# First stage of an attention and FFN kernel: V weights loaded as float32 and cast by GpSimd, x four buffers deep, norms pipelined, second V group from tile 17

## The chip, the cores and the metric

One Trainium2 chip, all 8 cores. Two cores share one sequence of the batch of four: the even core of a pair runs one plan, the odd core another. The metric is device time in microseconds of the slowest core of an execution, and the median over several executions.

Engine names: PE is TensorE's matmuls, PEld its weight loads, DVE is VectorE, ACT is ScalarE, POOL is GpSimd, SP is SyncE, which here only starts DMAs.

## The reference

```python
def _L0_attn_ref(x, Wq, bq, Wk, bk, Wv, bv, Wo, bo):      # 16 heads of 128, causal
    q = jnp.einsum('btc,hcd->bhtd', x, Wq) + bq[None, :, None, :]
    k = ...; v = jnp.einsum('btc,hcd->bhtd', x, Wv) + bv[None, :, None, :]
    scores = jnp.einsum('bhtd,bhsd->bhts', q, k) * scale
    probs = jax.nn.softmax(scores + causal, axis=-1)
    y = jnp.einsum('bhts,bhsd->bhtd', probs, v)
    return y.transpose(0, 2, 1, 3).reshape(Bn, Tn, H * D) @ Wo + bo
...
x = x + _layernorm(_L0_attn_ref(_layernorm(x), Wq, bq, Wk, bk, Wv, bv, Wo, bo))
x = x + _layernorm(_L0_ffn_ref(_layernorm(x), weight, w_scale, bias))   # int8 weights, x quantized per token
```

x is 4 x 4096 x 2048 in float32. The change touches only the inner layernorm of x, its transposition and the product with Wv.

## The kernel before

Each core works on token tiles of 128 rows. The even core's plan holds 21 tiles (NK = 21) and computes the output of all of them; the odd core's plan holds 32 tiles (NK = 32) for keys and values and computes the output of 11. The slowest core is an even one.

**The first stage**, the one that the change touches, goes over the tiles t = 0, 1, 2, ... For each one:
- SP starts the load of 128 rows of x, float32, 1 MB, into one of three buffers `xin` (`load_x`);
- DVE takes the statistics (`x_stats`: four BATCH_NORM_STATS2 of 128x512, one BATCH_NORM_AGGREGATE into the only `mv`), then waits for ACT's square root in `c_sd`, then makes the reciprocal `c_rs` and the shift `c_nm`;
- ACT takes the square root (L909), normalizes the tile into `xln` (L914, 128x2048, bf16, two buffers) and, once PE has transposed it, copies two halves from PSUM into `xT` (L919);
- PE transposes the tile in 16 blocks (`transposes`, L694), one tile ahead of its products, and computes V for it (`v_job`, L708): 16 matmuls of 512 columns per group of four heads;
- DVE adds the bias and evicts it (`v_out`, L1065) and SP stores it to DRAM (`store_v`).

V has four groups of 512 columns. Groups 0 and 1 belong to the first stage: group 0 is computed for each tile as it comes, group 1 beside it from tile `V2_AT` on (10 here), and then for the tiles before `V2_AT`. After that come K and Q of head 0, V groups 2 and 3, and then the heads, one after another, and the FFN; in all of this PE works from `xT` and the later weights.

**Orders written out by hand.** Every engine has one list of instructions, so the place of a step in it decides what it waits behind. ACT's list for one tile is: square root of t, normalization of t, the two copies of t. DVE's is: `v_out(0, t)`, then the whole of `x_stats(t + 3)`. PE's is: transposes of t + 1, `v_job(0, t)`, and from `V2_AT` on `v_job(1, t)`. SP's is: `load_x(t + 4)`, `store_v(0, t)`. `ps` has two banks for V jobs, `xln` and the statistics behind `c_sd` one or two buffers.

**V weights.** They lie in DRAM as float32. GpSimd starts the DMAs of a group in four parts (`load_wv`, L585), each 1 MB in DRAM, which the DMA itself casts to bf16 on the way into `wv[0]` or `wv[1]`. Group 0's four are started when the first x tile has landed; group 1's four after normalizations 1, 3, 5 and 7; the weights of Q and K of head 0 (`load_wqk(0)`, L599 and L600, 2 MB in DRAM) right behind them.

Of the kernel before, what the change touches and what calls it, by code (L numbers as in the profile page):

```python
# [28 lines left out]
V2_AT = 10  # L29


class Plan:
# [177 lines left out]
    def frees(self, lo, hi):  # L210
# [29 lines left out]
        + ["x_in%d" % i for i in range(3)]  # L240
# [26 lines left out]
def build_nc():  # L267
# [26 lines left out]
    with contextlib.ExitStack() as top:  # L294
# [44 lines left out]
        xin = at("xin", [128, 3, C], F32, A + 32 * KB)  # L339
# [91 lines left out]
        def sync_program(sp, pl):  # L431
# [36 lines left out]
            def load_x(t):  # L468
                if t >= 3:
                    w.wait_ge("ln_a", t - 2)  # L470
                sp.dma_start(out=xin[:, t % 3, :], in_=x_seq[t * 128:(t + 1) * 128, :]
                             ).then_inc(S["x_in%d" % (t % 3)], 16)
# [18 lines left out]
            load_x(3)  # L491
            for t in range(NK):
                if t + 4 < NK:
                    load_x(t + 4)
# [84 lines left out]
        def gpsimd_program(g, pl):  # L579
# [103 lines left out]
        def tensor_program(pe, pl):  # L683
# [19 lines left out]
            def v_job(grp, t):  # L703
                b = open_job(pl.job_no[("v", grp, t)])
                w.wait_ge("tp_ev", 2 * t + 2)
                for kc in range(KC):
                    w.wait_ge("wv%d%d" % (grp % 2, kc // 4), 16 * (grp // 2 + 1))
# [194 lines left out]
        def scalar_program(a, pl):  # L902
            w = Seen(a, S)
            NK, NQ, NC, N = pl.NK, pl.NQ, pl.NC, pl.N
            for t in range(NK):
# [3 lines left out]
                a.activation(c_sd[:, :], mv[:, 1:2], AF.Sqrt, bias=eps[:, :]).then_inc(S["sd_a"], 1)  # L909
# [3 lines left out]
                w.wait_ge("x_in%d" % (t % 3), 16 * (t // 3 + 1))  # L913
                a.activation(xln[:, t % 2, :], xin[:, t % 3, :], AF.Identity,  # L914
                             bias=c_nm[:, t % 4:t % 4 + 1], scale=c_rs[:, t % 4:t % 4 + 1]
                             ).then_inc(S["ln_a"], 1)
                for u in (2 * t, 2 * t + 1):
# [3 lines left out]
                                 ).then_inc(S["tp_ev"], 1)  # L921

# [83 lines left out]
        def vector_program(v, pl):  # L1006
# [21 lines left out]
            stats = {"a": 0, "c": 0}  # L1028
# [22 lines left out]
            def x_stats(t):  # L1051
                w.wait_ge("x_in%d" % (t % 3), 16 * (t // 3 + 1))
                if t >= 1:
                    w.wait_ge("nm_a", t)
                if t >= 4:
                    w.wait_ge("ln_a", t - 3)
                norm_of(xin[:, t % 3, :], t, "a")
# [405 lines left out]
```

## Time and profile before

| | us |
|---|---|
| median of 3 executions (lowest, highest) | 2204.31 (2201.59, 2579.76) |
| the profiled execution | 2206.36 |
| its span on core 0, the slowest | 2204.6 |
| spans of cores 2, 4, 6 | 2198.6, 2198.2, 2197.1 |
| spans of cores 1, 3, 5, 7 | 2152.3, 2148.3, 2149.1, 2147.8 |
| PE busy on core 0 | 2077.2 (94%) |
| DVE, ACT, POOL busy on core 0 | 1380.4, 1003.0, 244.9 |

All times of the rows are of core 0, from the start of its span, unless a row is of another core. A row of the timeline or of the chain begins with the start and the duration; "x4" is a count of instructions that were put together; what stands in square brackets is the idle time of that engine before the row, and what ended it. The GB/s of a stretch counts the bytes that arrive, so that a load that is cast from float32 to bf16 on the way counts half of what it reads.

### The profile page before, as it was taken

How to read it: one execution, taken by the hardware profiler on the slowest of the kernel's cores; microseconds unless marked ns; L12 is line 12 of the kernel's file. 1: busy time of each engine (PE TensorE's matmuls, PEld its weight loads, DVE VectorE, ACT ScalarE, POOL GpSimd, SP SyncE). 2: the span in 40 equal slices, each digit the busy share in tenths (PEclk: the TensorE clock that was granted, in tenths of full speed). 3: DMA queues.
4: the chain of work that ended last, by engine and by line, in shares of the span. 5: the costliest groups of instructions: out<-in, count | busy, mean ns of one | idle time of the engine just before them, and what ended most of it. 6: DMA issues, size and time to landing. Idle time of an engine off the chain costs nothing.

```text
span 2204.6 us, 35276 instructions; the slowest of 8 cores (2147.8 to 2204.6 us)
## 1 busy us (share of the span) xinstructions
PE 2077.2 (94%) x11037; PEld 973.5 (44%) x11252; DVE 1380.4 (63%) x2403; ACT 1003.0 (45%) x1437; POOL 244.9 (11%) x444
## 2 busy tenths in 40 slices
PE   4799999999999999999999999998899999999997
PEld 2354444444444444444444444444344444444443
DVE  3552322466776676676667766776577777777776
ACT  4650000466556555655565565556633333333332
POOL 0000100010011011101100110013001111111111
PEclk8999999999999999999999999999999999999998
DMA  8743312110221122012202210255443333333332
GB/s 210 219 149 78 70 40 63 38 40 11 43 41 27 26 41 43 14 37 43 42 10 43 43 40 11 43 99 135 152 146 113 108 115 115 115 115 105 100 104 77
DMA packets 167392, 168.67 MB, mean 77 GB/s; under 512 B 135842, under 2 KB 146594, under 8 KB 158498
## 3 DMA queue, kind: packets, MB, share of 16 engines
q1 hardware_dynamic: 157412, 124.38, 18.5%
q0 software_dynamic: 9792, 41.95, 9.4%
q8 instruction: 99, 1.62, 0.3%
q14 instruction: 89, 0.73, 0.1%
HBM read 140.61 MB, written 44.04 MB: 84 GB/s over the span
## 4 chain that ended last, share of the span: by engine, by line
PE 81%; DVE 9%; issue 5%; DMA 3%; ACT 2%; DVEq 0%; POOL 0%; SPq 0%; ACTq 0%; POOLq 0%
PE ps L721 22%; PE ps L708 12%; PE ps L896 12%; PE ps L880 11%; PE ps L756 9%; PE ps L773 7%; PE ps L787 3%; DVE rb L1149 2%; DVE rb L1147 1%; DMA wv<-wv_p 1%; PE ps L815 1%; DMA xin<-x_seq 1%; DVE hi L1135 1%; PE ps L797 1%; DVE lo L1137 1%
## 5 line engine op out<-in xcount | busy, mean ns | idle before, releaser
L946 ACT ACTIVATE P<-ps,negb 128x512 bf16<-128x512 f32 (+2 forms) x1104 | 677.8, 617 | 478.5 <-PE ps L756 465.6
L721 PE MATMUL ps<-xT,wqk 128*128 128x384 bf16 (+1 forms) x2997 | 736.8, 353 | 3.5
L721 PEld LDWEIGHTS ps<-xT,wqk 128*128 128x128 bf16 x3072 | 297.0, 98 | 259.4 <-issue 3.0
L756 PE MATMUL ps<-kq 128*128 128x512 bf16 (+2 forms) x1086 | 376.2, 346 | 11.9 <-ACT P L946 10.2
L773 PE MATMUL ps<-P,v_sb 128*128 128x512 bf16 (+3 forms) x1072 | 366.6, 344 | 20.6 <-DVE P L1127 19.0
L708 PE MATMUL ps<-wv,xT 128*128 128x512 bf16 x1312 | 296.8, 384 | 9.8 <-DMA wv<-wv_p 7.8
L896 PE MATMUL ps<-xT,qx 128*128 128x512 bf16 x1317 | 291.8, 379 | 1.4
L880 PE MATMUL ps<-xT,yj 128*128 128x512 bf16 x1191 | 274.6, 380 | 1.3
L708 PEld LDWEIGHTS ps<-wv,xT 128*128 128x128 bf16 x1344 | 131.7, 99 | 166.1 <-issue 17.5
L896 PEld LDWEIGHTS ps<-xT,qx 128*128 128x128 bf16 x1344 | 131.5, 98 | 158.6
L1080 DVE TENSOR_SCALAR kq<-ps,bqk 128x384 bf16<-128x384 f32 (+1 forms) x192 | 131.0, 683 | 87.0 <-PE ps L721 86.3
L880 PEld LDWEIGHTS ps<-xT,yj 128*128 128x128 bf16 x1216 | 119.3, 98 | 144.4 <-issue 2.0
L1147 DVE RECIPROCAL rb<-ps 128x192 f32<-128x192 f32 (+1 forms) x96 | 149.2, 1554 | 50.3 <-PE ps L798 49.9
L756 PEld LDWEIGHTS ps<-kq 128*128 128x128 bf16 x1104 | 107.8, 98 | 156.6 <-issue 76.6
L1065 DVE TENSOR_TENSOR vst<-ps,bvb 128x512 bf16<-128x512 f32 x84 | 58.1, 692 | 182.0 <-PE ps L708 181.7
L773 PEld LDWEIGHTS ps<-P,v_sb 128*128 128x128 bf16 x1104 | 108.1, 98 | 136.0 <-issue 41.5
L679 POOL TENSOR_TENSOR fo<-fo,fb 128x512 f32<-128x512 f32 x80 | 100.9, 1273 | 531.0 <-DVE fo L1247 531.0
L954 ACT ACTIVATE c_sd<-mv,eps 128x1 f32<-128x1 f32 x63 | 18.6, 294 | 286.8 <-DVE mv L1033 286.8
L1127 DVE TENSOR_TENSOR P<-P,tri 128x128 bf16<-128x128 bf16 x336 | 73.1, 225 | 119.6 <-ACT P L946 116.0
L1149 DVE RECIPROCAL rb<-ps 128x192 f32<-128x192 f32 (+1 forms) x96 | 145.2, 1512 | 0.0
L608 POOL TENSOR_TENSOR bt<-qm,km 128x1 f32<-128x1 f32 x96 | 18.4, 192 | 984.7 <-DVE km L1117 978.3
L946 ACT ACT_TABLE_LOAD x1 | 1.3, 1283 | 232.7 <-DMA v_g<-vst 232.7
(91 smaller groups left out, 1713.6 us busy)
## 6 DMA issues: line engine op xcount, KB each, us to landing
xin<-x_seq SPq DMA_DIRECT2D x21, 1024.0 KB, 6.1
x<-x_seq SPq DMA_DIRECT2D x21, 1024.0 KB, 5.0
out<-x SPq DMA_DIRECT2D x20, 1024.0 KB, 3.8
v_g<-vst SPq DMA_DIRECT2D x84, 128.0 KB, 1.7
v_sb<-v_g SPq DMA_DIRECT2D x16, 672.0 KB, 4.8
yj<-yt_h SPq DMA_DIRECT2D x21, 512.0 KB, 5.8
wv<-wv_p POOLq DMA_DIRECT2D x16, 512.0 KB, 10.5
wqk<-wq_p POOLq DMA_DIRECT2D x16, 512.0 KB, 5.2
```

The costliest lines, as they stand in the source:

```text
L679: g.tensor_tensor(part, part, fb[:, n * 512:(n + 1) * 512], ALU.add).then_inc(S["fb_ok"], 1)
L708: mm = pe.matmul(ps[:, b, :], xt_cols(pl, t, 1, kc), wv[grp % 2][:, kc, :], start=(kc == 0), stop=(kc == KC - 1))
L721: mm = pe.matmul(ps[:, JOB + job % 2, 0:n * 128], wqk[p][:, 0 if kind == "q" else 1, kc, :], xt_cols(pl, a, n, kc), start=(kc == 0), stop= ...
L756: pe.matmul(ps[:, S_BANK + s % 2, q0 * 128:n * 128], k_cols(pl, h, kt, 1), q_cols(pl, h, a + q0, n - q0), start=True, stop=True).then_inc( ...
L773: pe.matmul(ps[:, Y_BANK + n % 2, q0 * 128:m], v_sb[h % 2][:, kt, :], P[:, s % RP, q0 * 128:m], start=(v == 0), stop=(v == len(pl.keys[c]) ...
L880: mm = pe.matmul(ps[:, n, :], yj[:, j % 2, hc, :], wo_cols(n, hc), start=False, stop=(hc == H - 1))
L896: mm = pe.matmul(ps[:, n if j == NQ - 1 else 4 + n, :], qx(pl, j)[:, kc, :], w8_cols(n, kc), start=(kc == 0), stop=(kc == KC - 1))
L946: a.activation(P[:, s % RP, q0 * 128:m], ps[:, S_BANK + s % 2, q0 * 128:m], AF.Exp, bias=negb[:, k:k + 1], scale=SCALE).then_inc(S["exp_ok ...
L1080: v.tensor_scalar(dst, ps[:, JOB + job % 2, 0:n * 128], bqk[:, b:b + 1], None, ALU.add).then_inc(S["job_ev"], 1)
L1127: v.tensor_tensor(blk, blk, tri[:, :], ALU.mult).then_inc(S["mask_ok"], 1)
L1147: v.reciprocal(rb[:, 0:m // 2], ps[:, MISC, 0:m // 2]).then_inc(S["rec_ok"], 1)
L1149: v.reciprocal(rb[:, m // 2:m], ps[:, MISC, m // 2:m]).then_inc(S["misc_rd"], 1)
```

## The change

Four things, all in the first stage:
- **V weights of groups 0 and 1** go as plain float32 loads on SP's queue into a buffer `stage` (four parts of 128x2048 float32, laid in the upper part of `xT`, which holds tiles 24 and up), and GpSimd casts each part into `wv` with a `tensor_copy`. Group 0's four parts stand between the loads of x0, x1 and x2; group 1's four are started at tiles 5, 8, 11 and 14. GpSimd starts `load_wqk(0)` after the last normalization.
- **x loads** have four buffers and are started five tiles ahead.
- **Norms**: `x_stats` is cut into `x_begin` (statistics, into one of two `mva`) and `x_end` (reciprocal and shift). DVE's list becomes `v_out(0, t)`, `x_end(t + 3)`, `x_begin(t + 4)`. ACT's becomes: the copies of t, normalization of t + 1, square root of t + 2. A square root on `warm` stands first on ACT.
- **Second group** from tile 17: `V2_AT = 17`.

```diff
-V2_AT = 10
+V2_AT = 17
...
+        xin = [at("xin%d" % i, [128, C], F32, A + o * KB) for i, o in enumerate((32, 40, 48, 76))]
+        stage = at("stage", [128, 4, 4 * 512], F32, base + 24 * KC * 128 * 2)
...
             def load_x(t):
-                if t >= 3:
-                    w.wait_ge("ln_a", t - 2)
+                if t >= 4:
+                    w.wait_ge("ln_a", t - 3)
...
+            def load_wv(grp, k):
+                if grp == 1:
+                    w.wait_ge("wc", k + 1)
+                sp.dma_start(out=stage[:, k, :], in_=wv_p[grp, :, k * 2048:(k + 1) * 2048]
+                             ).then_inc(S["ws%d" % k], 16)
...
             load_x(0)
             sp.dma_start(out=ident[:, :], in_=masks_in[:, 0:128]).then_inc(S["id_in"], 16)
+            load_wv(0, 0)
+            load_wv(0, 1)
             load_x(1)
+            load_wv(0, 2)
+            load_wv(0, 3)
+            load_x(2)
             load_bv(0)
-            load_x(2)
+            load_x(3)
+            load_x(4)
...
             for t in range(NK):
-                if t + 4 < NK:
-                    load_x(t + 4)
+                if t + 5 < NK:
+                    load_x(t + 5)
+                if t in (5, 8, 11, 14):
+                    load_wv(1, (t - 5) // 3)
...
-            w.wait_ge("x_in0", 16)
-            for k in range(4):
-                load_wv(0, k)
-            for k in range(4):
-                w.wait_ge("ln_a", 1 + 2 * k)
-                load_wv(1, k)
+            for grp in range(2):
+                for k in range(4):
+                    w.wait_ge("ws%d" % k, 16 * (grp + 1))
+                    g.tensor_copy(wv[grp][:, 4 * k:4 * k + 4, :],
+                                  stage[:, k, :].rearrange("p (k n) -> p k n", n=512)
+                                  ).then_inc(S["wc"], 1)
+            w.wait_ge("ln_a", pl.NK)
             load_wqk(0)
...
+            w.wait_ge("cst", 1)
+            a.activation(warm[:, :], eps[:, :], AF.Sqrt)
+            deviation_a(0)
+            normalize(0)
+            for t in range(NK):
+                if t == 24:
+                    w.wait_ge("wc", 8)
                 for u in (2 * t, 2 * t + 1):
                     w.wait_ge("tp_mm", u + 1)
                     a.activation(xt_half(pl, t, u % 2),
                                  tp[:, u % 4, :].rearrange("p (k n) -> p k n", n=128), AF.Copy
                                  ).then_inc(S["tp_ev"], 1)
+                if t < 3:
+                    deviation_a(t + 1)
+                if t + 1 < NK:
+                    normalize(t + 1)
+                if 2 <= t < NK - 2:
+                    deviation_a(t + 2)
...
             for t in range(3):
-                x_stats(t)
+                x_begin(t)
+                x_end(t)
             for t in range(NK):
                 v_out(0, t)
+                if t == 0:
+                    x_begin(3)
                 if t + 3 < NK:
-                    x_stats(t + 3)
+                    x_end(t + 3)
+                if t + 4 < NK:
+                    x_begin(t + 4)
```

## Rows read from the trace of the kernel before

**Rows 1.** The page, core 0: the chain that ended last, by engine and by line

```profile
PE 81%; DVE 9%; issue 5%; DMA 3%; ACT 2%; DVEq 0%; POOL 0%; SPq 0%; ACTq 0%; POOLq 0%
PE ps L721 22%; PE ps L708 12%; PE ps L896 12%; PE ps L880 11%; PE ps L756 9%; PE ps L773 7%; PE ps L787 3%; DVE rb L1149 2%; DVE rb L1147 1%; DMA wv<-wv_p 1%; PE ps L815 1%; DMA xin<-x_seq 1%; DVE hi L1135 1%; PE ps L797 1%; DVE lo L1137 1%
```

**Rows 2.** Core 0, busy time of each engine in four stretches; last: clock, DMA share, GB/s

```profile
0.00:37.80 37.80, 10.35 (x51) 5.52 (x51) 11.21 (x37) 12.10 (x11) 3.58 (x10) 0.88 0.91 224
37.80:97.90 60.10, 43.89 (x283) 23.50 (x286) 34.76 (x75) 38.36 (x36) 2.11 (x4) 0.93 0.81 231
97.90:217.70 119.80, 119.04 (x660) 59.06 (x674) 48.74 (x96) 39.84 (x38) 2.12 (x4) 1.00 0.39 115
217.70:2204.60 1986.90, 1903.94 (x10048) 885.45 (x10242) 1285.73 (x2197) 912.68 (x1352) 237.08 (x426) 0.99 0.25 67
```

**Rows 3.** Core 0, the chain that ended last in 0 to 320 us, in order of time

```profile
10.08 25.71 DMA wv<-wv_p
...
35.93 1.88 PE ps L708 x4
...
38.57 2.47 DVE bn L1045 x4
...
42.58 2.10 ACT xln L914
...
75.43 16.06 DMA xin<-x_seq
...
97.97 1.05 PE tp L694 x16
...
105.93 0.89 PE tp L694 x16
...
213.02 4.70 PE ps L708 x21
```

**Rows 4.** Core 0, timeline of the start

```profile
7.81 2.47 DVE L1045 BATCH_NORM_STATS2 bn<-xin 128x6 f32<-128x512 f32 x4 [2.57 <-DMA xin<-x_seq]
```

**Rows 5.** Core 0, timeline of one tile before tile 10

```profile
67.33 2.09 ACT L914 ACTIVATE xln<-xin,c_nm,c_rs 128x2048 bf16<-128x2048 f32 x1 [0.73 <-DVE c_nm L1038]
68.45 0.69 DVE L1065 TENSOR_TENSOR vst<-ps,bvb 128x512 bf16<-128x512 f32 x1 [1.27 <-PE ps L708]
69.06 2.46 DVE L1045 BATCH_NORM_STATS2 bn<-xin 128x6 f32<-128x512 f32 x4
...
69.57 1.05 PE L694 MATMUL tp<-ident,xln 128*128 128x128 bf16 x16 [1.29 <-ACT xln L914]
...
70.27 1.94 ACT L919 ACTIVATE xT<-tp 128x1024 bf16<-128x1024 bf16 x2 [0.85 <-PE tp L694]
...
72.09 0.29 ACT L909 ACTIVATE c_sd<-mv,eps 128x1 f32<-128x1 f32 x1
...
73.12 2.09 ACT L914 ACTIVATE xln<-xin,c_nm,c_rs 128x2048 bf16<-128x2048 f32 x1 [0.74 <-DVE c_nm L1038]
```

**Rows 6.** Core 0, timeline of DVE: two evictions while PE is never idle

```profile
179.90 0.69 DVE L1065 TENSOR_TENSOR vst<-ps,bvb 128x512 bf16<-128x512 f32 x1 [2.76 <-PE ps L708]
183.36 0.69 DVE L1065 TENSOR_TENSOR vst<-ps,bvb 128x512 bf16<-128x512 f32 x1 [2.76 <-PE ps L708]
```

**Rows 7.** Stretches as in rows 2: core 0, plain loads alone

```profile
5.00:10.00 5.00, 0.00 (x0) 0.00 (x0) 2.37 (x6) 0.00 (x0) 1.66 (x3) 1.00 1.00 397
```

**Rows 8.** Stretches of core 1, the neighbour of core 0, from the start of its own span

```profile
5.00:10.00 5.00, 0.00 (x0) 0.00 (x0) 1.87 (x16) 0.00 (x0) 0.00 (x0) 1.00 0.05 10
...
15.00:20.00 5.00, 0.00 (x0) 0.00 (x0) 2.74 (x5) 1.19 (x1) 2.32 (x4) 1.00 0.98 306
```

**Rows 9.** Core 0, x tiles: time from a DMA's issue to its landing

```profile
DMA to landing us min/median/max: 4.9/6.1/16.1
```

**Rows 10.** Core 0, groups of GpSimd's instructions: busy, mean ns of one

```profile
L679 POOL TENSOR_TENSOR fo<-fo,fb 128x512 f32<-128x512 f32 x80 | 100.9, 1273 | 531.0 <-DVE fo L1247 531.0
...
L669 POOL CAST bohl<-bof 1x2048 bf16<-1x2048 f32 x1 | 2.2, 2160 | 0.1
```

More of the change, by code:

```diff
@@ L239 @@
         + ["wv%d%d" % (s, k) for s in range(2) for k in range(4)] + ["bv%d" % g for g in range(NG)]
-        + ["x_in%d" % i for i in range(3)]
+        + ["x_in%d" % i for i in range(4)] + ["ws%d" % i for i in range(4)] + ["wc"]
         + ["bn_a", "sd_a", "rs_a", "nm_a", "ln_a", "tp_mm", "tp_ev"]
@@ L338, in build_nc @@
         wv = [at("wv%d" % s, [128, KC, 512], BF16, A + 16 * KB * s) for s in range(2)]
-        xin = at("xin", [128, 3, C], F32, A + 32 * KB)
+        xin = [at("xin%d" % i, [128, C], F32, A + o * KB) for i, o in enumerate((32, 40, 48, 76))]
+        stage = at("stage", [128, 4, 4 * 512], F32, base + 24 * KC * 128 * 2)
+        mva = at("mva", [128, 2, 2], F32, small + 2880)
+        warm = at("warm", [128, 1], F32, small + 2912)
         xln = at("xln", [128, 2, C], BF16, A + 56 * KB)
@@ L706, in v_job @@
                 for kc in range(KC):
-                    w.wait_ge("wv%d%d" % (grp % 2, kc // 4), 16 * (grp // 2 + 1))
+                    if grp < 2:
+                        w.wait_ge("wc", 4 * grp + kc // 4 + 1)
+                    else:
+                        w.wait_ge("wv%d%d" % (grp % 2, kc // 4), 16)
                     mm = pe.matmul(ps[:, b, :], xt_cols(pl, t, 1, kc), wv[grp % 2][:, kc, :],
@@ L904, in scalar_program, with deviation_a @@
             NK, NQ, NC, N = pl.NK, pl.NQ, pl.NC, pl.N
-            for t in range(NK):
+            def deviation_a(t):
                 w.wait_ge("ag_a", t + 1)
@@ L908, in scalar_program, with normalize @@
                     w.wait_ge("rs_a", t)
-                a.activation(c_sd[:, :], mv[:, 1:2], AF.Sqrt, bias=eps[:, :]).then_inc(S["sd_a"], 1)
+                a.activation(c_sd[:, :], mva[:, t % 2, 1:2], AF.Sqrt, bias=eps[:, :]
+                             ).then_inc(S["sd_a"], 1)
+            def normalize(t):
                 w.wait_ge("nm_a", t + 1)
@@ L1026, in vector_program @@
             last.then_inc(S["cst"], 1)
-            stats = {"a": 0, "c": 0}
+            stats = {"c": 0}
             def norm_end(parts, i, tag):
@@ L1049, in norm_of, with x_begin, x_end @@
                 norm_end(bn6, i, tag)
-            def x_stats(t):
-                w.wait_ge("x_in%d" % (t % 3), 16 * (t // 3 + 1))
+            def x_begin(t):
+                w.wait_ge("x_in%d" % (t % 4), 16 * (t // 4 + 1))
                 if t >= 1:
-                    w.wait_ge("nm_a", t)
+                    w.wait_ge("ag_a", t)
+                if t >= 2:
+                    w.wait_ge("nm_a", t - 1)
+                    w.wait_ge("sd_a", t - 1)
+                for k in range(4):
+                    v.bn_stats(bn6[:, k, :], xin[t % 4][:, k * 512:(k + 1) * 512]
+                               ).then_inc(S["bn_a"], 1)
+                w.wait_ge("bn_a", 4 * t + 4)
+                v.bn_aggr(mva[:, t % 2, :], bn6[:, :, :]).then_inc(S["ag_a"], 1)
+            def x_end(t):
+                b = t % 4
+                w.wait_ge("sd_a", t + 1)
                 if t >= 4:
                     w.wait_ge("ln_a", t - 3)
-                norm_of(xin[:, t % 3, :], t, "a")
+                v.reciprocal(c_rs[:, b:b + 1], c_sd[:, :]).then_inc(S["rs_a"], 1)
+                w.wait_ge("rs_a", t + 1)
+                v.tensor_scalar(c_nm[:, b:b + 1], mva[:, t % 2, 0:1], c_rs[:, b:b + 1], -1.0,
+                                ALU.mult, ALU.mult).then_inc(S["nm_a"], 1)
             def v_out(grp, t):
```

9 lines of the change are left out of this document (4 added, 5 removed).

## The prediction

> **What bounds the kernel now.** I read the chain of waits first, then the busy time in stretches, then the timeline of the first stage. The chain is PE for 81% of the span, and its lines for loads are at 1% each [rows 1]: whatever the first stage loses is small beside the whole. The stretches say how small. Behind 217.7 us, where the second V group is finished, PE is busy 1904 of 1987 us with work that waits for nothing of the first stage but its end; so what the first stage gains or loses goes straight into core 0's time [rows 2]. Up to 37.8 us PE is busy 10.4 us, from there to 97.9 us 43.9 of 60.1, and from 97.9 to 217.7 us all the time [rows 2].
>
> What PE has to do in the stage: one V job is 183.36 - 179.90 = 3.45 us where PE is never idle [rows 6], one tile's transposes are 0.89 us, 0.9 with rounding, where a job's matmuls follow them [rows 3], so 42 x 3.45 + 21 x 0.9 = 163.8 us. The stage ends at 213.02 + 4.70 = 217.7 [rows 3]. It loses 54 us, and that is the most that any change of it can give: 2.4% of the kernel. The loss has three parts:
> - The first V job waits for the last part of the weights, which lands 25.7 us after its issue, and ends at 37.8 [rows 3].
> - Up to tile 10 a tile takes 73.12 - 67.33 = 5.79 us, where PE's own work is 3.45 + 0.9 = 4.35. The loop runs through ACT: a normalization (2.09), 0.85 until the first transposes are there, two copies (72.09 - 70.27 = 1.82 until the next instruction), the square root, and then 1.03 from its start until the next normalization begins, because ACT sits idle for DVE's reciprocal and shift (0.73 to 0.74) [rows 5].
> - One x tile takes 16.1 us to land where 6.1 is the median, behind cast weight loads [rows 3, 9].
>
> **The change part by part.** *V weights and x loads, the start.* All is now one queue, in order. x0 lands at 7.7 as before: DVE's first statistics start at 7.81 [rows 4]. The rate of plain loads on core 0 is 397 GB/s while its neighbour moves 10 [rows 7, 8], and 306 on core 1 when both load, with cast loads among them that count half [rows 8]. A part of 1.05 MB takes 2.6 us by the one and 3.4 by the other. I take 2.6 for the first (the neighbour is still silent) and, as the nearest row holds undercounted casts, the middle, 3.0, for those after it. Landings: weights part 0 at 10.3, part 1 at 13.3, x1 at 16.3, parts 2 and 3 at 19.3 and 22.3, x2 at 25.3, and with 0.26 MB of bias x3 at 29.1, x4 at 32.1.
>
> The Trainium skill, page "DMA: Bandwidth & Descriptors", section Bandwidth, says that with both cores of an HBM domain streaming each gets about 358 GB/s. By that figure 1.05 MB is 2.93 us and x2 would come at 25.0, by the row of 397 at 23.5; the rows of this trace don't decide, since no stretch has plain loads alone on both cores.
>
> *GpSimd's cast* of 128x2048 is not in the trace. From below stands a cast of 2048 elements on one partition, 2.16 us; from above a two-input operation on 128x512, 1.27 us, times four, 5.1 us [rows 10]. It has one input, so I take 3. A cast then keeps up with the loads, and the last is done at 25.3. At 5.1 the four run end to end from 10.3 to 30.7; the matmuls behind the last would end at about 32.6 instead of some 30 and push the transposes of tile 2 by 1.1 us. Both ends are in the range. Nothing stands behind the casts on GpSimd's queue but the weights of Q and K of head 0, which now start after the last normalization, near 125 us, with 60 us of V jobs before they are wanted: nothing.
>
> *From x to normalized.* From the start of the statistics to the end of the normalization it is 44.68 - 38.57 = 6.1 us [rows 3]. So tile 1 is normalized at 22.4 and tile 2 at 31.4. PE transposes tile 1 from 22.5 to 24.4 (twice 0.9 and a little, taking half clock) and runs the first V job from 24.4 to at most 31.2 at half clock, where four matmuls take 1.88 us [rows 3]: it ends before tile 2 is wanted, so here the clock costs nothing. The first V job is thus done some 7 to 9 us earlier than at 37.8, and tile 2's copies end at 31.4 + 0.85 + 1.82 = 34.1. Its square root for tile 3 follows, and tile 3 is normalized at 34.1 + 1.03 + 2.09 = 37.2. DVE takes tile 4's statistics only behind the shift of tile 3, from 35.1 to 37.9, so the copies of tile 3 start at 38.3 and tile 4 is normalized at 42.2. The square root on `warm` moves ACT's table load ahead of tile 0, which waits for weights either way: nothing.
>
> *The loop up to tile 17.* ACT no longer waits for DVE: the next square root stands two tiles ahead and falls into the 0.85 us that the transposes take anyway. What is left of the loop is 0.85 + 1.82 + 2.09 = 4.76 us [rows 5]; with one more semaphore step I take 4.8. Who is late next: PE needs 0.15 (69.57 - 69.42) + 0.9 + 3.45 = 4.5; DVE 0.6 until behind an eviction and 2.47 of statistics [rows 5], and for its three short instructions some 1.0, an estimate from the 1.03 in which ACT's root, the reciprocal and the shift all fit: 4.1. So ACT sets it, by 0.3 us. Loads per tile are 1.05 MB of x, 0.13 MB of V stored, and a third of 1.05 MB of weights between tiles 5 and 14: 1.53 MB, or 4.4 us at 350 GB/s. An x load is issued after the eviction of tile t - 1 and the normalization of t + 1, and read two evictions later, 9.6 us, against 6.1 to land [rows 9] and 3.0 where a weights part is ahead of it. That is covered by half a microsecond, the thinnest cover of the change; if it is gone, up to 1 us is lost at each of four tiles.
>
> *Second group from tile 17.* It moves PE work behind the loop and removes none. For seven more tiles PE has one job per tile and idles 4.8 - 4.35 = 0.45 us at each, 3 us, which is in the sum below; in return the four loads of group 1 are spread over ten tiles, and nothing waits for them: the last is issued at tile 14, near 95 us, lands 3 to 9 us later and is cast by 110, and the first job of group 1 stands at 109.4 + 0.15 + 0.9 + 3.45 = 113.9.
>
> *The sum.* Tile 18 is normalized at 42.2 + 14 x 4.8 = 109.4. From there PE is never idle: 0.15, three tiles' transposes (2.7) and 4 + 21 = 25 jobs (86.3). The stage ends at 198.5 instead of 217.7: 19.2 us less. The same sum on the trace of before checks it: from 97.97 there are 10 transposes and 32 jobs, 9.0 + 110.4 = 119.4, and the trace has 119.7 [rows 3]. The profiled execution, span 2204.6 and time 2206.36, would be 2187.2; it lies 2.05 above the median of 2204.31, so the median becomes 2185. The even cores stay the slowest, by some 50 us.
>
> **The rivals.**
> *The loop doesn't get shorter.* DVE's statistics of tile t + 4 now stand ahead of the next eviction, and ACT's square root behind a normalization; if either hand-over misses its slot the old 5.79 comes back. For it: DVE's cover is only 0.7 us. Then tile 18 is at 42.2 + 14 x 5.79 = 123.3 and the stage ends at 212.4: 5 us less, 2199.
>
> *The queue becomes the bound (the slower side).* The mechanism: everything that tile 18 needs, 19 x tiles, 8 parts of weights, bias and 17 stores of V, 31.6 MB, goes through the queue before it, where the cast loads brought half the bytes into SBUF. It decides below the rate at which tile 18 is later than 128.6 us, the time that gives back all 19.2: with 5 us before the first bytes and 7 behind the last, 31.6 MB in 116.6 us, 271 GB/s. Against it stands 397 [rows 7]; for it the stretch up to 97.9, where the mean was 231 at 0.81 of the engines [rows 2]. At 231 the tile comes at 149 us and the stage ends near 238: 2224. Only a rate under 197 GB/s would cost over 2%.
>
> *GpSimd and DVE block each other.* Eight casts of 3 us run beside DVE's statistics. If each held DVE up for its whole length, the four of the start would delay tile 2 by about 3 us and the four of the loop, against 0.7 of cover, by 2.3 each: 12 us in all, and the gain is 7, 2197. For it: the two share the work of the stage here for the first time, and no row has a GpSimd operation on 128 partitions beside statistics. The Trainium skill, page "SBUF — State Buffer", section "Who interferes with whom", says that a DVE instruction with at most one SBUF input outside the two-port modes doesn't contend with GpSimd; the statistics and the eviction have one each. By that rule this rival falls; that the short shift instruction has two costs it 0.2 us at a time.
>
> *The start gains more.* If the rate stays at 397 for both cores, x2 lands 1.8 earlier, and if PE rather than ACT sets the loop (4.5), tile 18 is at 103: 2179.
>
> **How the numbers follow.** The forecast of 2185, with 2180 to 2192 for its own unknowns (rate, cast), has 0.6; the old loop, 2199, 0.15; blocking, 2197, 0.06; the queue, 2200 to 2224, 0.07; the better start, 2172 to 2179, 0.12. Leaving out 2 in 10, half of the better start and the queue's upper end among them, gives 2176 to 2201. Faster by over 2% means under 2160, a gain of 44 of the 54 us that are there, 0.02; slower by over 2% needs a rate that no row has, 0.02. 2% is about what a measurement of this kernel can tell from no change.
>
> **What would show it.** In the profile after: the first eviction near 29 to 31 us (37.8 before, at the end of the first stretch of rows 2); GpSimd casts of 2.2 to 5.1 us; ACT's normalizations 4.8 us apart between tiles 5 and 17 with no idle time put down to the shift `c_nm`; x landings of 6 us, no 16; no wait of DVE's statistics for x behind tile 4; saturated PE from 109 us; the K and Q work of head 0 from 198 us. It is wrong if normalizations are further apart than 5 us, if statistics wait for x in the loop, or if the part behind the stage changes its length.

## The result and the profile after

The changed kernel takes 2187.35 us (median of six executions; the kernel before 2204.36 beside them). The ratio is 0.9925, 95% interval 0.9914 to 0.9936: 16.5 us less. The forecast was 2185. Executions in which the cores of one die were slowed are left out of every ratio here; the medians count them.

The stage ends where PE starts the first K or Q product of head 0. On the four even cores that was 217.6, 213.1, 212.4 and 214.6 us before (mean 214.4), and is 198.1, 199.0, 198.4 and 199.1 now (mean 198.6): 15.8 us less. From there to the end of the span the four cores take 1985.2 us in the mean before and 1983.7 now. So the first stage gave the gain.

Core 6, the slowest of the profiled execution, in order of time: the chain that ended last, in 0 to 300 us (start, duration, what).

```profile
6.08 18.79 DMA xin<-x_seq
25.09 2.48 DVE bn L1098 x4
...
86.44 11.45 DMA xin<-x_seq
98.13 2.48 DVE bn L1098 x4
...
110.13 1.05 PE tp L713 x16
...
199.30 3.03 PE ps L743 x18
```

The weights are gone from the chain [rows 3]. It begins with the load of x2 and goes over ACT up to tile 18, whose normalization is followed by the transposes at 110.13; from there it is PE, and the chain's first K and Q products stand at 199.3 (the first of all starts at 199.1). One late x tile (11.45 us) is still in it.

The timeline of the start, core 6:

```profile
7.69 2.47 DVE L1098 BATCH_NORM_STATS2 bn<-xin 128x6 f32<-128x512 f32 x4 [2.65 <-DMA xin<-x_seq]
10.26 1.89 POOL L643 CAST wv<-stage 128x2048 bf16<-128x2048 f32 x1 [9.56 <-DMA stage<-wv_p]
...
15.24 2.47 DVE L1098 BATCH_NORM_STATS2 bn<-xin 128x6 f32<-128x512 f32 x4 [3.74 <-DMA xin<-x_seq]
...
21.80 1.89 POOL L643 CAST wv<-stage 128x2048 bf16<-128x2048 f32 x1 [1.75 <-DMA stage<-wv_p]
...
23.16 5.24 PE L730 MATMUL ps<-wv,xT 128*128 128x512 bf16 x16
25.09 2.47 DVE L1098 BATCH_NORM_STATS2 bn<-xin 128x6 f32<-128x512 f32 x4 [5.98 <-DMA xin<-x_seq]
...
31.26 2.47 DVE L1098 BATCH_NORM_STATS2 bn<-xin 128x6 f32<-128x512 f32 x4 [1.21 <-DMA xin<-x_seq]
```

The brackets name what DVE waited for: x0 at 7.7, x1 at 15.2, x2 at 25.1, x3 at 31.3. The casts take 1.89 us and are through at 23.7; the first V job runs from 23.2 to 28.4, before tile 2 wants PE, and its eviction starts at 29.4 (36.9 on this core before, 37.97 on core 0).

The timeline of one tile in the loop, core 6, against [rows 5]:

```profile
61.26 0.29 ACT L931 ACTIVATE c_sd<-mva,eps 128x1 f32<-128x1 f32 x1
62.22 1.94 ACT L952 ACTIVATE xT<-tp 128x1024 bf16<-128x1024 bf16 x2 [0.67 <-PE tp L713]
64.04 2.09 ACT L939 ACTIVATE xln<-xin,c_nm,c_rs 128x2048 bf16<-128x2048 f32 x1
66.03 0.29 ACT L931 ACTIVATE c_sd<-mva,eps 128x1 f32<-128x1 f32 x1
```

The normalization no longer has a wait in brackets: ACT's idle 0.73 us for the shift is gone, the square root lies in the time of the transposes, and a tile takes 66.03 - 61.26 = 4.77 us (5.79 before). What is left is 0.67 us of waiting for PE.

Busy time in stretches, core 6 and then its neighbour, core 7, each from the start of its own span (the last three columns are clock, share of the DMA engines, GB/s):

```profile
20.00:25.00 5.00, 3.50 (x21) 2.41 (x22) 0.00 (x0) 3.29 (x3) 1.94 (x2) 1.00 0.97 255
...
60.00:80.00 20.00, 18.85 (x132) 9.96 (x132) 15.37 (x34) 17.34 (x17) 3.17 (x2) 1.00 0.99 318
80.00:98.00 18.00, 16.85 (x123) 9.13 (x124) 12.11 (x27) 15.34 (x17) 2.51 (x2) 1.00 0.98 321
```

```profile
60.00:80.00 20.00, 18.95 (x134) 9.99 (x133) 13.76 (x31) 17.34 (x18) 1.89 (x1) 1.00 0.98 285
80.00:98.00 18.00, 16.17 (x121) 8.66 (x119) 14.73 (x32) 14.67 (x15) 1.89 (x1) 1.00 0.99 345
```

PE is busy 18.85 of 20 us where it was 43.9 of 60.1 [rows 2]. And the DMA engines are at 0.98 to 0.99: with plain loads only, the two cores get 603 and 666 GB/s together, 302 and 333 each in the mean of the two. The granted clock is 1.00 in all these rows. In the whole stage it is at half (1.2 instead of 2.4 GHz) at most once on an even core, for 3.4 us that end by 35.6 us. Before, it was at half for 6.8 to 10.2 us between 29 and 39 us and again once or twice behind 40 us, on core 0 at 46.0 to 49.5 and 90.4 to 93.8.

### The profile page after: what moved, and what is told of

It reads as the page before. It is cut to its first block, busy times and chain, and to the rows that moved or that the text cites. A ratio compares the mean times of both kernels' runs of the same rounds, so it can differ in the third digit from the quotient of the medians.

```text
span 2183.7 us, 35313 instructions; the slowest of 8 cores (2134.3 to 2183.7 us)
## 1 busy us (share of the span) xinstructions
PE 2071.6 (95%) x11038; PEld 970.4 (44%) x11252; DVE 1380.1 (63%) x2403; ACT 1002.4 (46%) x1438; POOL 256.0 (12%) x444
## 4 chain that ended last, share of the span: by engine, by line
PE 81%; DVE 8%; issue 5%; ACT 3%; DMA 2%; DVEq 0%; SPq 0%; POOL 0%; ACTq 0%; POOLq 0%
PE ps L743 22%; PE ps L918 12%; PE ps L902 11%; PE ps L730 11%; PE ps L778 9%; PE ps L795 8%; PE ps L809 3%; DVE rb L1203 2%; DVE rb L1201 1%; DMA xin<-x_seq 1%; PE ps L837 1%; ACT xln L939 1%; ACT P L985 1%; PE ps L819 1%; DVE lo L1191 1%
## 5 line engine op out<-in xcount | busy, mean ns | idle before, releaser
L778 PE MATMUL ps<-kq 128*128 128x512 bf16 (+2 forms) x1086 | 376.5, 347 | 11.9 <-ACT P L985 10.1
L730 PE MATMUL ps<-wv,xT 128*128 128x512 bf16 x1313 | 292.2, 380 | 1.7 <-issue 0.2
```

The costliest lines, as they stand in the source:

```text
L730: mm = pe.matmul(ps[:, b, :], xt_cols(pl, t, 1, kc), wv[grp % 2][:, kc, :], start=(kc == 0), stop=(kc == KC - 1))
L778: pe.matmul(ps[:, S_BANK + s % 2, q0 * 128:n * 128], k_cols(pl, h, kt, 1), q_cols(pl, h, a + q0, n - q0), start=True, stop=True).then_inc( ...
```

## The experiments

Twelve kernels: eight of them in the table beside the two that are compared, four further down. The stage's end is the mean over the four even cores of one profiled execution; each core's lies within 4 us of it. The ratio is to the kernel before on the same chip. The column "Q, K loads" says when GpSimd starts `load_wqk(0)`: early is behind group 1's weights, at 59 to 65 us, late is behind the last normalization.

| | norms | x buffers | weights | Q, K loads | second group from | stage ends, us | ratio (95%) |
|---|---|---|---|---|---|---|---|
| before | old | 3 | cast in DMA | early | 10 | 214.4 | 1 |
| only `V2_AT` | old | 3 | cast in DMA | early | 17 | 227.3 | 1.0067 (1.0044 to 1.0090) |
| only the norms | new | 3 | cast in DMA | early | 10 | 226.1 | 1.0052 (1.0026 to 1.0078) |
| weights and buffers | old | 4 | plain | late | 10 | 207.1 | 0.9964 (0.9953 to 0.9976) |
| norms and buffers | new | 4 | cast in DMA | late | 10 | 202.5 | 0.9934 (0.9911 to 0.9957) |
| changed, old norms | old | 4 | plain | late | 17 | 217.3 | 1.0015 (1.0004 to 1.0025) |
| changed, cast in DMA | new | 4 | cast in DMA | late | 17 | 206.0 | 0.9960 (0.9947 to 0.9973) |
| changed, three buffers | new | 3 | plain | late | 17 | 209.4 | 0.9998 (0.9964 to 1.0033) |
| changed, second group from 10 | new | 4 | plain | late | 10 | 198.1 | 0.9942 (0.9921 to 0.9963) |
| **changed** | new | 4 | plain | late | 17 | 198.6 | 0.9925 (0.9914 to 0.9936) |

The ratio follows the stage's end within its interval: 12.9 us later gives 14.8 +- 5 us more, 7.3 earlier gives 7.9 +- 3 less.

The late start of the loads for Q and K is part of the change, but no run undoes or makes it alone. Where a kernel with early loads is set beside one with late loads, it is in the difference.

### One part undone

**The norms in the old order**, the rest as changed:

```diff
-            deviation_a(0)
-            normalize(0)
             for t in range(NK):
+                deviation_a(t)
+                normalize(t)
...
-                if t < 3:
-                    deviation_a(t + 1)
-                if t + 1 < NK:
-                    normalize(t + 1)
-                if 2 <= t < NK - 2:
-                    deviation_a(t + 2)
...
-                if t == 0:
-                    x_begin(3)
                 if t + 3 < NK:
+                    x_begin(t + 3)
                     x_end(t + 3)
-                if t + 4 < NK:
-                    x_begin(t + 4)
```

> The changed kernel with the old order of the norms (ACT: root, normalization, copies of one tile; DVE: statistics, reciprocal and shift of tile t + 3 in one piece), all else as changed. Theory (the order of the norms is what shortens the loop): normalizations are 5.79 us apart again instead of 4.77, 14 tiles up to tile 18, so the stage ends 14 us later, near 213, and the time is near 2201, ratio to the kernel before 0.998 to 1.000. Rival (the loop was long because loads of x and weights collided, and plain loads cured it): normalizations stay under 5 us apart and the time is within 3 us of 2187.

2208.99 us, more than the kernel before. Its timeline (core 2):

```profile
86.93 0.29 ACT L931 ACTIVATE c_sd<-mva,eps 128x1 f32<-128x1 f32 x1
...
88.03 2.09 ACT L939 ACTIVATE xln<-xin,c_nm,c_rs 128x2048 bf16<-128x2048 f32 x1 [0.80 <-DVE c_nm L1104]
...
92.79 0.29 ACT L931 ACTIVATE c_sd<-mva,eps 128x1 f32<-128x1 f32 x1
```

A tile takes 5.86 us again, with 0.80 of waiting for the shift. The rival (plain loads cured the loop) falls: x is never late in this kernel behind tile 3, and the loop is as long as before. The expectation was right in kind and short in size: the stage ends at 217.3 and not 213, and the time is 2209 and not 2201.

Part of what is missing stands in the granted clock. Cores 0 and 4 keep 1.00 through the stage and end the stage at 214.9 and 215.1. Cores 2 and 6 have the same loop, but the clock falls to half for 3.4 us, four times on one and three on the other, and behind each time one tile takes 7.0 to 7.4 us; they end at 220.6 and 218.7. One such stretch on core 2, a V job in it (3.62 us at full clock), and the same stretch on core 0:

```profile
44.00:51.00 7.00, 6.39 (x37) 3.33 (x38) 2.00 (x7) 4.68 (x5) 0.00 (x0) 0.76 0.72 243
45.81 4.98 PE L730 MATMUL ps<-wv,xT 128*128 128x512 bf16 x16
```

```profile
44.00:51.00 7.00, 5.29 (x40) 2.87 (x39) 4.75 (x10) 5.13 (x5) 0.00 (x0) 1.00 0.67 190
```

PE had been idle for 2.5 us before the transposes in front of this V job. Why the clock falls on two cores and not on two others with the same loop is not shown. In the changed kernel PE is idle less and no even core has it at half behind 35.6 us.

**The weights cast by the DMA**, from GpSimd's queue with the old gates:

```diff
-            load_wv(0, 0)
-            load_wv(0, 1)
             load_x(1)
-            load_wv(0, 2)
-            load_wv(0, 3)
             load_x(2)
...
-            for grp in range(2):
-                for k in range(4):
-                    w.wait_ge("ws%d" % k, 16 * (grp + 1))
-                    g.tensor_copy(wv[grp][:, 4 * k:4 * k + 4, :], ...
+            w.wait_ge("x_in0", 16)
+            for k in range(4):
+                load_wv(0, k)
+            for k in range(4):
+                w.wait_ge("ln_a", 1 + 2 * k)
+                load_wv(1, k)
             w.wait_ge("ln_a", pl.NK)
             load_wqk(0)
```

> The changed kernel with the V weights of groups 0 and 1 loaded by GpSimd's casting DMAs with the gates of before (after x0; after normalizations 1, 3, 5, 7), all else as changed. Theory (the weights' place in the order of loads sets the start): the first V job ends near 37.8 us again instead of 29, the copies of tile 2 and all behind them come 5 to 6 us later, and group 1's and Q's and K's loads (started early) collide with x once more, 3 to 8 us: stage end 208 to 212, time 2196 to 2201. Rival (the bytes are the same, only the queue differs): first V job within 2 us of 29, time within 3 us of 2187.

2194.0 us; the stage ends at 206.0, 2 us before the lower end of what was expected. The expectation counts on early loads for Q and K, but the edit leaves them behind the last normalization. The chain of its start (core 4):

```profile
9.94 25.50 DMA wv<-wv_p
35.58 1.88 PE ps L721 x4
38.23 2.47 DVE bn L1087 x4
```

The last weights land at 35.4 (35.8 on core 0 before), and tile 3's normalization starts at 41.9 instead of 35.4 in the mean of the even cores: 6.5 of the 7.4 us by which the stage ends later. The rival (the bytes are the same) falls. The 7.4 us are what the order of the loads, the one queue and the plain loads are worth together; the run does not separate them.

**Three x buffers**, loads four tiles ahead:

```diff
             def load_x(t):
-                if t >= 4:
-                    w.wait_ge("ln_a", t - 3)
+                if t >= 3:
+                    w.wait_ge("ln_a", t - 2)
...
-            load_x(3)
-            load_x(4)
...
+            load_x(3)
-                if t + 5 < NK:
-                    load_x(t + 5)
+                if t + 4 < NK:
+                    load_x(t + 4)
```

> The changed kernel with three x buffers and loads four tiles ahead, all else as changed. Theory (the loads are now covered only by the fourth buffer): a load is issued behind the eviction of tile t - 1 and read behind that of t, so two tiles take 0.8 + landing (6.5 to 9) + 2.8 us, 5.05 to 6.3 per tile instead of 4.77, and the stage ends 4 to 17 us later, most likely 10: 2197. Rival (landing is covered anyway): normalizations 4.77 apart, time within 3 us of 2187.

2199.53 us. Statistics wait for x at 11 to 15 tiles on each even core, 0.4 to 4.2 us at a time, and the stage ends 10.8 us later: the 10 of the expectation. The ratio's interval is wide because one execution of 2226 us is in it; the others in it lie between 2197.5 and 2199.7.

**The second group from tile 10**, its weights at tiles 1, 3, 5 and 7:

```diff
-V2_AT = 17
+V2_AT = 10
...
-                if t in (5, 8, 11, 14):
-                    load_wv(1, (t - 5) // 3)
+                if t in (1, 3, 5, 7):
+                    load_wv(1, (t - 1) // 2)
```

> The changed kernel with the second group from tile 10 on, and its weights at tiles 1, 3, 5 and 7, all else as changed. Theory A (PE idles 0.42 us at each of seven more tiles if the second group comes late): PE is saturated from about 75 us on, 3 us less, and the late x tile of 1.6 us is hidden as well: 2183. Theory B (the queue is the thinner thing: 1.70 MB per tile at 320 GB/s are 5.3 us): statistics wait for x between tiles 3 and 9 and the 3 to 5 us are lost again: 2187 to 2190.

2190.99 us, with an interval that overlaps the changed kernel's; the stage ends at 198.1 against 198.6. Statistics wait for x where the weights are ahead of it (core 4):

```profile
72.00 2.48 DVE L1098 BATCH_NORM_STATS2 bn<-xin 128x6 f32<-128x512 f32 x4 [3.33 <-DMA xin<-x_seq]
...
82.41 2.47 DVE L1098 BATCH_NORM_STATS2 bn<-xin 128x6 f32<-128x512 f32 x4 [2.06 <-DMA xin<-x_seq]
```

Both theories have a part: PE is saturated earlier (A), and the queue takes that back (B). The run moves the weights together with the tile, so the two are weighed as a pair: in the changed kernel this pair is worth nothing that can be measured. Tile 17 by itself is another matter. With casting loads, which start at the same places in both kernels, the new order of the norms and four buffers, the stage ends at 206.0 with tile 17 and at 202.5 with tile 10 (table): 3.4 us, near the 3 us of PE idling that the prediction counts.

### One part alone

**Only the second group from tile 17**, in the kernel before:

```diff
-V2_AT = 10
+V2_AT = 17
```

> The kernel before with the second group from tile 17 alone. Theory: seven more tiles take 5.79 us at 4.35 of work for PE, 10 us more: 2214, ratio 1.0045. Rival (the later start hides nothing and costs nothing, since PE's work is the same): 2204.

2220.77 us. The stage ends 12.9 us later, 10 of it as expected; where the other 2.9 come from is not separated. The late x tiles at 79 to 84 us (3.0 to 4.4 us of waiting) are there as in the kernel before, and on cores 0 and 4 the granted clock falls to half three more times, for 3.4 us each, between 98 and 132 us. So tile 17 costs 13 us with the long loop. With the short one it costs 3.4 us under casting loads, and nothing where group 1's plain weights move along with it.

**Only the order of the norms**, in the kernel before; ACT's list is that of the change, and DVE's:

```diff
...
             for t in range(NK):
                 v_out(0, t)
-                if t + 3 < NK:
-                    x_stats(t + 3)
+                if t == 0:
+                    x_begin(3)
+                if t + 3 < NK:
+                    x_end(t + 3)
+                if t + 4 < NK:
+                    x_begin(t + 4)
                 if t >= V2_AT:
                     v_out(1, t)
```

> The kernel before with the new order of the norms alone (three x buffers, casting weight loads, second group from tile 10). Theory (a shorter loop needs the fourth buffer and the freed queue): x tiles are read one loop after they are issued, landing 6 to 9 us, so a tile takes 5.05 to 6 us instead of 5.79 up to tile 10, and the late tiles of 8 and 16 us stay: 0 to 6 us less, most likely 3: 2201. Rival (the parts add up: the order of the norms alone is worth the 20 us that undoing it cost): 2190 or less.

2217.52 us: slower by 11.5 us, which neither theory had. The rival (the parts add up) falls, and my own theory named the right cause and missed its worst effect. DVE's timeline (core 4) and PE's of the same stretch, where PE should be saturated:

```profile
107.97 0.15 DVE L1086 RECIPROCAL c_rs<-c_sd 128x1 f32<-128x1 f32 x1
108.23 0.21 DVE L1088 TENSOR_SCALAR c_nm<-mva,c_rs 128x1 f32<-128x1 f32 x1
113.51 2.48 DVE L1076 BATCH_NORM_STATS2 bn<-xin 128x6 f32<-128x512 f32 x4 [5.06 <-DMA xin<-x_seq]
...
116.27 1.28 DVE L1097 TENSOR_TENSOR vst<-ps,bvb 128x512 bf16<-128x512 f32 x2
```

```profile
111.58 3.62 PE L710 MATMUL ps<-wv,xT 128*128 128x512 bf16 x16
117.09 3.61 PE L710 MATMUL ps<-wv,xT 128*128 128x512 bf16 x16 [1.90 <-DVE vst L1097]
```

With three buffers the load of x is issued one eviction before it is read. DVE's list puts the statistics of tile t + 4 ahead of the eviction of group 1's job, DVE stands 5.1 us in front of them, the job's bank isn't emptied, and PE waits 1.9 us at each tile of a stretch in which it never waited. Tiles are mostly 9 to 11 us apart there instead of 7.8. From 107 us on these waits are 10 to 12 us on each even core, about as much as the stage ends later (11.7).

Before tile 10 there is a wait of 10 us for one x tile as well, behind the early loads of Q's and K's weights:

```profile
59.48 0.54 POOL L601 DMA_DIRECT2D wqk<-wq_p  x1
60.00 0.55 POOL L602 DMA_DIRECT2D wqk<-wk_p  x1
...
75.94 2.48 DVE L1076 BATCH_NORM_STATS2 bn<-xin 128x6 f32<-128x512 f32 x4 [10.08 <-DMA xin<-x_seq]
```

The two land at 69.3 and 75.4; the x tile behind them is issued at 61.8 and lands at 75.7. The tile of 16.1 us in the kernel before lies there too: it is issued at 75.4 while the loads of Q and K, issued at 64.7 and 65.2, are under way until 83.6. In the two kernels with casting V weights, four buffers and late loads for Q and K no x tile keeps the statistics waiting longer than 1.9 us between 58 and 83 us.

**Norms and four buffers**, casting weight loads with the old gates: the kernel with the casting DMAs from above, and

```diff
-V2_AT = 17
+V2_AT = 10
```

> The kernel before with the new order of the norms and four x buffers, casting weight loads with the old gates, second group from tile 10. Theory (the fourth buffer is what the norms alone lacked): a tile takes 4.77 us up to tile 10 except where x is late behind weight loads (70 to 82 us), the eviction of the second group is no longer held by statistics that wait for x, and the stage ends near 205: 2193. Rival (the casting loads on a second queue spoil it): as the norms alone, 2205 or more.

2190.61 us, the stage ends at 202.5 (205 expected). The +11.7 us of the norms alone have become -11.9. Two things differ from that kernel, the fourth buffer and the late start of Q's and K's weights. PE's waits for the eviction from 107 us on, 10 to 12 us, are gone. They are about half of the difference of 24 us, and they belong to the buffers, since the loads for Q and K had long landed there. How the other half divides between the buffer and those loads is not shown; the 10 us wait for one tile was behind them.

**Weights and four buffers**: the kernel with the old norms from above, and

```diff
-V2_AT = 17
+V2_AT = 10
...
-                if t in (5, 8, 11, 14):
-                    load_wv(1, (t - 5) // 3)
+                if t in (1, 3, 5, 7):
+                    load_wv(1, (t - 1) // 2)
```

> The kernel before with plain weight loads and casts and four x buffers, but the old order of the norms and the second group from tile 10 (its weights at tiles 1, 3, 5, 7). Theory (undoing the norms cost 20 us because tile 17 as the start of the second group makes 7 more tiles wait for the loop): with 5.86 us per tile tile 4 is normalized near 43 and tile 11 near 84, PE is saturated from there, and the stage ends near 204: 10 us less than before, 2194. Rival (only the norms matter): within 3 us of 2204.

2198.37 us; the stage ends at 207.1 us against the 204 expected. Core 0, whose granted clock is at 1.00 all through the loop, ends it at 203.4. Cores 2, 4 and 6 have tiles of 6.7 to 8.2 us before 83 us; their clock is at half four times, twice and once, and they end at 210.1, 206.7 and 208.3.

### The disputed costs, and what is left

**Each cast twice** on GpSimd.

```diff
+                    g.tensor_copy(wv[grp][:, 4 * k:4 * k + 4, :], ...).then_inc(S["wd"], 1)
+                    w.wait_ge("wd", 4 * grp + k + 1)
                     g.tensor_copy(wv[grp][:, 4 * k:4 * k + 4, :], ...
```

> The changed kernel with each of the eight casts done twice by GpSimd, one after the other. Theory (1.89 us per cast lies beside loads that come every 3 us, and GpSimd and DVE don't block each other): the first V job starts at most 2 us later but still before tile 2 wants PE, normalizations stay 4.77 us apart, the time is within 2 us of 2187. Rival (casts and DVE's statistics block each other): each added cast costs up to 1.9 us, statistics of 0.67 us stretch, the time is 5 to 15 us more.

Ratio 0.9926 (0.9892 to 0.9961), the stage ends at 198.7. From the views of the tiles `stage` and `xin` (core 4; duration in ns, least, median, most):

```profile
L643 POOL CAST wv<-stage x8: 1891/1896/1898, 10.1 to 107.9; 128x2048 bf16<-128x2048 f32 x8
L647 POOL CAST wv<-stage x8: 1896/1896/1898, 12.1 to 109.9; 128x2048 bf16<-128x2048 f32 x8
L1102 DVE BATCH_NORM_STATS2 bn<-xin x84: 675/677/697, 7.5 to 113.2; 128x6 f32<-128x512 f32 x84
```

Statistics take 677 ns, at most 697, and every cast 1.89 to 1.90 us, the doubled ones like the first. On each even core 14 to 20 of the 84 statistics run beside a cast, and they take 674 to 697 ns like the others. GpSimd and DVE don't block each other here, and the cast is hidden with 1.89 us to spare.

**Second group from tile 21:**

```diff
-V2_AT = 17
+V2_AT = 21
...
-                if t in (5, 8, 11, 14):
-                    load_wv(1, (t - 5) // 3)
+                if t in (16, 17, 18, 19):
+                    load_wv(1, t - 16)
```

> The changed kernel with the second group from tile 21 and its weights at tiles 16 to 19, nothing else. Theory: the late x tile near 82 to 98 us (0.9 to 2.3 us of waiting) is gone because no weights share the queue there, and three more tiles idle PE by 0.42 us each: within 1 us of 2187, stage end 198 to 200, with the engines' share of the queue under 0.9 between 60 and 98 us instead of 0.98. Rival (something else than weights made x late): the same waits remain and the time is 1 to 3 us more.

The profiled execution takes 2186.98 us and one other 2188.16, too few for an interval; the stage ends at 198.7. Core 6:

```profile
60.00:80.00 20.00, 18.85 (x131) 9.86 (x131) 15.15 (x34) 17.34 (x17) 0.00 (x0) 1.00 0.78 254
80.00:98.00 18.00, 16.85 (x123) 9.24 (x125) 14.43 (x31) 15.34 (x17) 0.00 (x0) 1.00 0.77 263
```

The share of the engines falls from 0.98 to 0.78, and no core waits for x behind 40 us. So it was group 1's weights that made x late.

**x ahead of the weights, transposes two tiles ahead of the V jobs**, statistics and x loads one tile further ahead:

```diff
-            load_wv(0, 0)
-            load_wv(0, 1)
             load_x(1)
-            load_wv(0, 2)
-            load_wv(0, 3)
             load_x(2)
+            load_wv(0, 0) ... load_wv(0, 3)
...
             transposes(0)
+            transposes(1)
             for t in range(NK):
-                if t + 1 < NK:
-                    transposes(t + 1)
+                if t + 2 < NK:
+                    transposes(t + 2)
```

> The changed kernel with the transposes two tiles ahead of the V jobs, DVE's statistics and the x loads one tile further ahead, and x1 and x2 loaded ahead of group 0's weights. Theory (what is left at the start is that ACT, which sets the loop, waits for x2 and so does nothing from 24 to 29 us): tile 2 is normalized at 23 instead of 31.6, tile 3 at 34.7 instead of 37.4, the first V job ends near 31, and PE has three tiles in stock and is nearly saturated from 28 us on: stage end near 192 instead of 199, time 2180. Rival (the weights are the bound of the start, and the loads of six tiles in a row push them out): first V job behind 33 us and time 2185 to 2190.

2196.53 us, 9 us slower than the changed kernel and above what either side expected. The first job ends at about 32 us; it is the second that is late (core 2):

```profile
28.19 4.26 PE L731 MATMUL ps<-wv,xT 128*128 128x512 bf16 x16
...
38.08 1.87 PE L714 MATMUL tp<-ident,xln 128*128 128x128 bf16 x16 [5.62 <-ACT xln L941]
```

PE's list has the transposes of tile 3 ahead of the second job, and the statistics of x3 start at 29.5 to 31.9, so PE stands 5.6 us with a job at hand. I had counted on three tiles in stock, but PE takes its list in order.

**ACT's normalization two tiles ahead of its copies** from tile 4, statistics and x loads one tile further ahead, and the weights as in the kernel with tile 21:

```diff
                 if t < 3:
                     deviation_a(t + 1)
-                if t + 1 < NK:
-                    normalize(t + 1)
-                if 2 <= t < NK - 2:
+                    normalize(t + 1)
+                if t in (2, 3):
                     deviation_a(t + 2)
+                if 2 <= t < NK - 2:
+                    normalize(t + 2)
+                if 3 <= t < NK - 3:
+                    deviation_a(t + 3)
```

> The changed kernel with ACT's normalization two tiles ahead of the copies from tile 4 on, DVE's statistics and the x loads one tile further ahead, the second group from tile 21 and its weights at tiles 16 to 19. Theory (ACT's 0.67 us of waiting for the transposes can be filled, and PE's 4.35 us then sets the loop once the queue carries only 1.18 MB per tile): tiles are 4.4 us apart from tile 5 to 17, and the stage ends near 193 instead of 198.6: 2181. Rival (the queue is the bound: at 320 GB/s landing takes longer than the 6.4 us that are left between issue and reading): statistics wait for x, tiles 4.8 us or more apart, 2187 or more.

2184.22 us, ratio 0.9897 (0.9862 to 0.9932), the stage ends at 195.2: 3.4 us before the changed kernel, 2 less than expected (the kernel with tile 21, which has the same weights, ends it at 198.7). PE on core 2:

```profile
67.40 1.06 PE L714 MATMUL tp<-ident,xln 128*128 128x128 bf16 x16
68.29 3.62 PE L731 MATMUL ps<-wv,xT 128*128 128x512 bf16 x16
...
71.75 1.06 PE L714 MATMUL tp<-ident,xln 128*128 128x128 bf16 x16
```

A tile takes 71.75 - 67.40 = 4.35 us, PE's own work. The first eviction comes at 35.6 us instead of 29.3, because DVE's list now has x3's statistics ahead of it; that is where the missing 2 us went, as far as the timeline shows. The ratio's interval overlaps the changed kernel's, so the gain is shown by the stage's end on all four even cores (194.6 to 195.9 against 198.1 to 199.1) and not by the time.

## Why the prediction was right, step by step

- *What bounds the kernel*: right. In all twelve kernels and the changed one the time moved with the end of the first stage, and what lies behind it kept its length within 4 us in the mean of the even cores.
- *Landings at the start*, by the start of the statistics on core 6: x1 at 15.2 (16.3 said), x2 at 25.1 (25.3), x3 at 31.3 (29.1). Between 10 and 15 us the rate was 426 GB/s on core 6, more than taken; then it fell to 255 GB/s between 20 and 25 us. The middle of the two rows hit x2, on which the sum hangs, because the two errors cancelled: that is luck. The figure of about 358 GB/s per core, from the page of the Trainium skill that the prediction names, was somewhat high: where both cores of a pair are at 0.98 to 0.99 of their engines, they have 302 and 333 each in the mean.
- *Cast*: 1.89 us, below the lower end of 2.16 to 5.1. My lower bound, one partition, was no bound. It changed nothing in the sum.
- *The first V job*: four matmuls in 1.88 us make sixteen in 7.5, which ends at 31.9 and not at 31.2, half a microsecond behind the normalization of tile 2. The slip cost nothing: the job started at 23.2 and took 5.2 us.
- *Loop*: 4.77 us, 4.8 said. ACT sets it, with 0.67 us idle for the transposes. This is the main step, and it held.
- *x loads in the loop*: the thin cover was right, its form not quite: three of four even cores wait for one tile behind a part of group 1's weights, 0.9 to 2.3 us (core 6 for a second, 0.4), and core 4 0.3 only, instead of up to 1 us at each of four tiles. The landings behind a part took up to 11.5 us where 9.1 was counted. In the sum this was nothing; on core 6 it cost 0.9 us, 5.7 us between two normalizations instead of 4.8. "Statistics wait for x in the loop" was one of the prediction's own signs of being wrong, and it came, as did x landings well over 6 us. It mattered little: a wait of 0.9 us cost nothing and one of 2.3 us cost 0.9: DVE had some 1.3 us to spare, where 0.7 was counted.
- *Tile 18 normalized* at 110.0 (109.4 said), stage end 199.1 (198.5).
- *The term that was mis-sized* is the start of the subtraction: 19.2 us was taken from core 0's stage of 217.7, but the other even cores ended theirs at 212.4 to 214.6, and in the changed kernel all four lie within 1 us. The mean gain is 15.8. The spans of cores 2, 4 and 6 stood beside core 0's, 6 us or more shorter; their stages should have been read too. Core 0 was behind core 4 by 5.2 us, and two differences make most of it: its first eviction came at 37.97 against 35.17, and one of its tiles took 7.36 us instead of 5.80, behind this V job (3.62 us at full clock) with the granted clock at half from 46.0 to 49.5 us (its chain before):

```profile
45.87 5.16 PE ps L708 x16
```

- *The loss of 54 us* had a part that the list of three leaves out. Behind 40 us the granted clock was at half for 3.4 to 6.9 us on each even core, and in the changed kernel it never is. At half clock at most half of that time is lost, so this is an estimate of up to 1.7 to 3.5 us of the gain.
- *The late tile of 16.1 us* was put down to cast weight loads. The V weights had all landed at 74.8 us, before it was issued; under way beside it were the loads for Q and K. The change moves these behind the last normalization, and the prediction counts that at nothing for what waits for them. What it gave to x was not asked, and no run shows it alone.
- *Second group from tile 17*: the 3 us of idling at seven more tiles stand in the stage's end as 0.5 against tile 10 with plain loads, where earlier weights delay x, and as 3.4 with casting loads.
- *The rivals*: the old loop came back only where the norms were in the old order. Blocking fell by the doubled casts. By the rule of the Trainium skill, page "SBUF — State Buffer", section "Who interferes with whom", a DVE instruction with at most one SBUF input, outside the two-port modes, does not contend with GpSimd, and the measured 677 ns agree. The queue was nearer than the 0.07 said: it decided below 271 GB/s, and core 6 had about 320 from 60 to 98 us with the engines all but full, 301 in the mean of 5 to 117 us.

What the prediction didn't ask is how the parts depend on each other. Undoing one part at a time costs 18.7 (norms), 10.8 (fourth buffer) and 7.4 us (weights) of the stage, 37 in all, where the whole gives 15.8; and two of the parts alone, the norms and tile 17, make the kernel slower. The other two were not run alone.

## What to carry to other kernels

- Where engines take hand-written lists in order, an operation moved forward needs its input to be there that much earlier: the new order of the norms with three buffers moved the stage's end by +11.7 us, with four, and Q's and K's weights loaded late, by -11.9. Count, for each step put ahead of another, what it can wait for, and who waits behind it.
- Judge an edit by undoing it and by doing it alone. The start of the second group at tile 17 cost 13 us in the kernel before and 3.4 us with the short loop and the same casting loads.
- Look at every step that an edit moves, also at one that "waits for nothing". The loads for Q and K had no one behind them, but they shared the DMA engines with x.
- Read the stage on every core that can be the slowest, not on the one that was, and its granted clock with it: cores with the same list of instructions ended the stage up to 7 us apart.

## What the runs showed of the hardware

- GpSimd's cast of 128x2048 from float32 to bf16 took 1.89 us, less than 2.16 for the same length on one partition [rows 10].
- Both cores of a pair loading plain float32 had 603 to 666 GB/s together at 0.98 to 0.99 of their DMA engines; alone at the start, one had 397 [rows 7].
- In kernels whose PE was idle 1.3 us or more of every tile, the granted clock fell to half for stretches of 3.4 us on some cores and not on others with the same instructions. A V job in such a stretch took 4.98 us instead of 3.62 (changed, old norms), and in the kernel with weights and buffers the stage ended at 210.1 us on core 2 (four such stretches) against 203.4 on core 0 (none).
